# Two groups of attention outputs in one PSUM bank, and a round of seven banks for all other jobs

## The chip, the cores and the metric

The kernel runs on one core of one Trainium2 chip. The metric is the device time of one execution in microseconds (us); lower is better. The names of the engines are those of the profile: PE is the matrix engine (PEld its weight loads), DVE the vector engine, ACT the scalar engine, POOL the third elementwise engine, SP the queue that issues DMAs. PSUM is the memory that PE writes its results to; the program holds it as one tensor `ps` of 128 partitions, 8 banks and 512 float32 values in each bank.

## The reference, cut to what matters

The input `x` is 8 images of 256 channels and 16x16 pixels. A non-local block and a quantised convolution block come first. Then the pixels become 256 tokens of 256 channels for each image, and four residual layers follow:

```python
t = t + _L2_attn_ref(_ln_t(t), L2_attn_w_in, L2_attn_b_in, L2_attn_w_out, L2_attn_b_out)
t = t + _L2_ffn_ref(_ln_t(t), L2_ffn_weight)
t = t + _L3_attn_ref(_ln_t(t), L3_attn_w_q, L3_attn_w_k, L3_attn_w_v, L3_attn_w_o)
t = t + _L3_ffn_ref(_ln_t(t), L3_ffn_We, L3_ffn_be, L3_ffn_Wr, L3_ffn_br, L3_ffn_Wo, L3_ffn_bo)
```

Both attentions are causal, with 16 heads of 16 channels:

```python
scores = jnp.einsum('bhqd,bhkd->bhqk', q, k) / math.sqrt(dh)   # the first one adds an alibi bias
scores = jnp.where(causal, scores, -inf)
attn = jax.nn.softmax(scores, axis=-1)
out = jnp.einsum('bhqk,bhkd->bhqd', attn, v)
```

The change touches only how the last line of this, the product of the softmax weights with V, is held in PSUM and copied out, and how many banks all other products of these four layers share.

## The kernel before

The first part of the program (the two convolution blocks, about 0 to 115 us) is not touched. The second part works through 16 bodies: 8 images through the first attention and its feed-forward layer (stages 0 and 1), then 8 images through the second attention and the mixture of experts (stages 2 and 3). A body is a list of pieces `(kind, stage, batch, n)`, each with a step in time; a body begins 12 steps after the one before, so that three or four images are under way at once. `in_order("tensor")` gives the order in which PE does the pieces, `in_order("others")` the order for ACT, DVE, POOL and SP. Each engine takes its pieces strictly in this order, and waits on semaphores.

The pieces, as far as the text needs them:

- `LNa`, `LNb`: the layer norm on DVE (statistics L1364 to L1370, and `xn` at L1375), with one power on POOL between them (L1079). `T`: PE turns `xn` around (L1119), ACT copies it to `xnT` (L1277).
- `Q`, `K`, `V` (L1127, L1135): the projections, taken out by ACT (L1291, L1294) and DVE (L1385, L1388, L1410, L1412).
- The 16 heads are 4 groups of 4. `S` (3 per group): scores, of which DVE takes the maximum (`nmax`, L1419). `MS`: DVE splits the maximum (L1428, L1429). `M`: PE turns it (L1183), ACT copies it into `QS` (L1306). `X` (3 per group): scores again, transposed and with the maximum taken off (L1194 begins them, L1198 ends them); ACT takes the exponential into `PT` (L1312).
- `O0` and `O1` (L1209, L1216): the product of V with `PT` for group n, with a row of sums. Four matmuls of 32 rows each fill the 128 partitions, 256 columns wide. ACT copies these to `OT` (L1316). `OX` (L1223): PE turns `OT` back, and DVE divides by the sums into `attn` (L1435, L1436).
- `AT`, `PR`: `attn` turned (L1119) and copied by ACT, projected (L1135) and added to the residual by DVE (L1446). `FF`: the feed-forward product (L1135), also added at L1446.
- `R`, `RT`, `GT`, `GB`, `E` (8 per image, L1252), `CT`: the router, its gates (transposed by PE at L1241, copied by ACT into `gateT` at L1327, used by PE at L1246), the experts, which DVE scales and adds up two by two (`acc`, L1499), and the output.

PSUM is shared as follows. All kinds in `JOBS` (all products named above but `O0` and `O1`) take a bank in turn, `self.bank[p] = jobs % RING` with `RING = 6`. Before it writes, PE waits until the previous job in the same bank is copied out, that is the job six places back in its own order: `drained(pe, piece, 1)`. Banks 6 and 7 are for the attention outputs, bank `6 + n % 2` for group n. Both groups of a pair (0 and 1, 2 and 3) stand at the same step, behind each other: `O0` and `O1` of the even group, then `O0` and `O1` of the odd one; their `OX` come two steps later.

Of the kernel before, what the change touches and what calls it, by code (L numbers as in the profile page):

```python
# [9 lines left out]
ACT = mybir.ActivationFunctionType  # L10
# [5 lines left out]
PIX = IMG * IMG  # L16
# [8 lines left out]
GROUPS = 4  # L25
# [37 lines left out]
                   ("br", 2 * EXPERTS))  # L63

UNITS = 3 * GROUPS
RING = 6

# [96 lines left out]
def signals(piece, bank):  # L166

    kind, n = piece[0], piece[3]
    out = []
    if kind in JOBS:  # L170
        out += [(f"bank_full{bank}", 1), (f"bank_drained{bank}", 1)]
    if kind == "O1":
        out += [(f"bank_full{6 + n % 2}", 1), (f"bank_drained{6 + n % 2}", 1)]
    if kind in SETTLED:
        out.append(("dve_step", settled(piece)))
    out += {"LNa": [("var_ready", 1), ("rstd_ready", 1)], "LNb": [("xn_ready", 1)], "XB": [("x_biased", 1)],
            "MS": [("max_split", 1)], "PAD": [("own_rows", 1), ("padded", 4), ("chosen", 1), ("chosen_spread", 16 * (STACKS - 1))], "CT": [("out_stored", 16)],
            "Q": [("first_ready0", 1)], "K": [("first_ready1", 1)],
            "SPLIT": [(f"second_ready{n}", 1), (f"third_ready{n}", 1), (f"parts_stored{n}", 16)],
            "LOAD": [(f"stack_loaded{n}", 16 * (len(Q_PARTS) + (piece[1] == 0 and n == 0)))],  # L180
            "R": [("router_shifted", 1)], "RT": {0: [("router_exp", 1)], 3: [("gates_ready", 1)]}.get(n, [])}.get(kind, [])
    return out
# [22 lines left out]
COUNTS = Counts()  # L205


def build(nc, x_in, fix_in, fixb_in, bias_in, w0_in, w1_in, wt_in, wm_in, parts_dram, out):
    ctx = ExitStack()
    with ctx:  # L210
# [6 lines left out]
        ps = ctx.enter_context(nc.psum_tensor("ps", [P, 8, 512], F32))  # L217
# [714 lines left out]
        with ExitStack() as c2:  # L932
# [23 lines left out]
            OT = lb("OT", [P, 2, PIX])  # L956
# [25 lines left out]
            def bank_number(piece):  # L982

                if piece is None:
                    return None
                return 6 + piece[3] % 2 if piece[0] == "O1" else COUNTS.bank.get(piece)

            def full(eng, piece):

                wait(eng, f"bank_full{bank_number(piece)}", piece)  # L990

            def drained(eng, piece, less=0):

                wait(eng, f"bank_drained{bank_number(piece)}", piece, less)
# [7 lines left out]
            def flat(ap):  # L1002
                return ap.rearrange("p a n -> p (a n)")
# [25 lines left out]
            def earlier_unit(kind, stage, batch, n, by, per):  # L1029

                return previous(kind, stage, batch, (n - by) % per, (by - n + per - 1) // per)
# [74 lines left out]
            def tensor_piece(pe, piece):  # L1106
# [6 lines left out]
                mm = None  # L1113
# [85 lines left out]
                                       QS[r, at, 4 * g + j, kt * P:], start=False, stop=(k == len(heads) - 1),  # L1199
                                       skip_group_check=True)  # L1200
                if kind == "O0":
                    o = ps[:, 6 + n % 2, :]
                    drained(pe, ("X", stage, batch, 3 * n))
                    drained(pe, ("X", stage, batch, 3 * n + 1))
                    if n == 0:
                        drained(pe, ("V", stage, batch, 0))
                    drained(pe, ("O1", stage, batch, n), 1)
                    for j in range(4):
                        pe.matmul(o[32 * j:32 * j + 32, 0:PIX], V[:, at, 0, 4 * n + j, :],  # L1209
                                  PT[:, pt_slot(piece, 3 * n + j // 2), (j % 2) * PIX:(j % 2 + 1) * PIX],  # L1210
                                  start=True, stop=False, skip_group_check=True)
                if kind == "O1":
                    o = ps[:, 6 + n % 2, :]
                    drained(pe, ("X", stage, batch, 3 * n + 2))
                    for j in range(4):
                        mm = pe.matmul(o[32 * j:32 * j + 32, P:PIX], V[:, at, 1, 4 * n + j, :],  # L1216
                                       PT[:, pt_slot(piece, 3 * n + 2), j * P:(j + 1) * P],
                                       start=False, stop=True, skip_group_check=True)
                    mm.then_inc(sems[f"bank_full{6 + n % 2}"], 1)
                if kind == "OX":  # L1220
                    drained(pe, ("O1", stage, batch, n))
                    for t in range(2):
                        mm = pe.transpose(d[:, t * P:(t + 1) * P], OT[:, n % 2, t * P:(t + 1) * P], F("ident"))  # L1223
                if kind == "AT":
# [46 lines left out]
            def scalar_piece(act, piece):  # L1271
# [37 lines left out]
                if kind == "X":  # L1309
                    full(act, piece)  # L1310
                    pt_free(act, piece)
                    act.activation(PT[:, pt_slot(piece, n), :], bank(piece), ACT.Exp).then_inc(drain(piece), 1)  # L1312
                if kind == "O1":
                    full(act, piece)
                    full(act, earlier_unit("OX", stage, batch, n, 2, GROUPS))
                    act.activation(OT[:, n % 2, :], ps[:, 6 + n % 2, 0:PIX], ACT.Copy)\  # L1316
                        .then_inc(sems[f"bank_drained{6 + n % 2}"], 1)
                if kind == "AT":
                    full(act, piece)
                    full(act, ("PR", stage, batch - 1, 0))  # L1320
# [15 lines left out]
            def pt_free(eng, piece):  # L1336

                earlier = earlier_unit("X", *piece[1:], PT_RING, UNITS)
                if earlier:
                    full(eng, ("O1", *earlier[1:3], earlier[3] // 3))  # L1340


            def vector_piece(dve, piece):
# [332 lines left out]
```

## Time and profile before

| what | value |
|---|---|
| median of 3 runs | 665.81 us (664.83 to 666.66) |
| the profiled execution's own time | 665.75 us |
| its span, first to last instruction | 664.0 us |
| around the span | 1.75 us |
| granted clock of PE, mean | 0.964 |
| PE busy | 593.3 us (89%) |
| DVE busy | 447.8 us (67%) |
| ACT busy | 326.7 us (49%) |

A granted clock of 1 is 2.4 GHz, 0.5 is 1.2 GHz. An engine's idle time matters where the chain of work that ends last runs through it.

### The profile page before, as it was taken

The page shows a single profiled execution, that of the slowest core. Times are in us where ns is not written, and L with a number is a line of the kernel's source. Part 1 is how long each engine was busy: PE and PEld are TensorE (multiplying, and loading weights), DVE is VectorE, ACT ScalarE, POOL GpSimd, SP SyncE. Part 2 cuts the span into 40 slices and gives each one's busy share as a digit, 9 for nine tenths or more (in the row PEclk, how much of TensorE's full clock was granted, in tenths as well). Part 3 has the DMA queues.
Part 4 walks back from the last instruction along what each step waited for, and adds up shares of the span by engine and source line. Part 5 has one row for each costly group of instructions (what it writes and reads, how often), then busy time and mean ns, then how long its engine had stood idle before and what let it go on. Part 6 is the DMA issues. An engine that isn't in the chain of part 4 may idle for free.

```text
span 664.0 us, 11227 instructions
## 1 busy us (share of the span) xinstructions
PE 593.3 (89%) x4159; PEld 407.7 (61%) x4206; DVE 447.8 (67%) x1275; ACT 326.7 (49%) x548; POOL 117.8 (18%) x115
## 2 busy tenths in 40 slices
PE   5884776768999999999999979999999999999897
PEld 2653334656767767767767757576675756565443
DVE  4767858758477577677677584776858576676464
ACT  2436658617566566566566554343443535353110
POOL 2031000260313313303303302011030200000000
PEclk9985998789899999999999988999999999999999
DMA  9500000375134134134134141204040230000000
GB/s 335 216 0 0 1 0 6 82 212 168 50 99 146 44 107 146 33 116 139 37 113 138 30 120 55 89 25 135 1 142 18 62 98 17 1 17 0 17 13 19
DMA packets 40253, 50.64 MB, mean 76 GB/s; under 512 B 4052, under 2 KB 33492, under 8 KB 39892
## 3 DMA queue, kind: packets, MB, share of 16 engines
q1 hardware_dynamic: 40200, 49.94, 24.3%
q8 instruction: 33, 0.54, 0.4%
q14 instruction: 20, 0.16, 0.1%
HBM read 35.11 MB, written 14.68 MB: 75 GB/s over the span
## 4 chain that ended last, share of the span: by engine, by line
PE 60%; DVE 15%; issue 3%; ACT 2%; DMA 1%; SPq 1%; POOL 0%; DVEq 0%; ACTq 0%
PE ps L1252 14%; PE ps L1135 8%; PE ps L1127 7%; PE ps L1209 5%; PE ps L1198 5%; DVE nmax L1419 4%; PE ps L1119 4%; PE ps L1194 3%; PE ps L1178 3%; PE ps L1170 3%; PE ps L1216 2%; DVE acc L1499 2%; PE ps L1173 2%; DVE xn L1375 2%; DVE stats L1364 2%
## 5 line engine op out<-in xcount | busy, mean ns | idle before, releaser
L1419 DVE TENSOR_REDUCE nmax<-ps 128x2 f32<-128x512 f32 (+1 forms) x192 | 130.7, 687 | 79.5 <-PE ps L1178 52.1
L1312 ACT ACTIVATE PT<-ps 128x512 f32<-128x512 f32 x192 | 113.3, 598 | 115.7 <-PE ps L1198 114.0
L1252 PE MATMUL ps<-wm,xnT 128*128 128x512 f32 x256 | 119.9, 599 | 0.7
L1079 POOL TENSOR_TENSOR rstd<-ve,fix 128x2 f32<-128x2 f32 x32 | 22.2, 695 | 321.6 <-DVE ve L1370 321.6
L1306 ACT ACTIVATE QS<-ps 8x1024 bf16<-8x1024 f32 x64 | 65.1, 1017 | 27.3 <-PE ps L1183 25.3
L1198 PE MATMUL ps<-QS,KS 110*128 110x256 bf16 (+3 forms) x512 | 74.7, 247 | 0.0
L1499 DVE SCALAR_TENSOR_TENSOR acc<-ps,gate,acc 128x256 f32<-128x256 f32 x128 | 61.6, 481 | 18.5 <-PE ps L1252 16.2
L1252 PEld LDWEIGHTS ps<-wm,xnT 128*128 128x128 f32 x256 | 45.1, 190 | 39.7 <-issue 38.1
L1127 PE MATMUL ps<-xnT,by_dim 128*128 128x256 f32 x256 | 63.4, 394 | 2.2 <-ACT xnT L1277 2.2
L1099 POOL TENSOR_TENSOR parts<-rest,fix 128x512 bf16<-128x512 f32 x30 | 38.1, 1270 | 139.8 <-DVE rest L1388 100.5
L1194 PE MATMUL ps<-fixb 128*128 128x256 bf16 (+1 forms) x192 | 60.0, 312 | 2.3 <-DVE nmax L1419 2.0
L1127 PEld LDWEIGHTS ps<-xnT,by_dim 128*128 128x128 f32 x256 | 48.0, 197 | 8.8 <-ACT xnT L1277 2.1
L1198 PEld LDWEIGHTS ps<-QS,KS 110*128 110x128 bf16 (+1 forms) x512 | 45.2, 98 | 11.9 <-issue 1.7
L1178 PE MATMUL ps<-KS,QS 110*128 110x256 bf16 (+1 forms) x256 | 50.1, 277 | 0.0
L1135 PE MATMUL ps<-wt,xnT 128*128 128x256 f32 x192 | 45.8, 381 | 0.0
L1209 PE MATMUL ps<-PT,V 128*32 128x256 f32 x512 | 41.9, 400 | 0.0
L1135 PEld LDWEIGHTS ps<-wt,xnT 128*128 128x128 f32 x192 | 34.8, 190 | 4.1
L1173 PE MATMUL ps<-fixb 128*128 128x256 bf16 x128 | 35.7, 279 | 1.0 <-DVE rest L1385 1.0
L1103 POOL TENSOR_TENSOR parts<-rest,parts 128x512 bf16<-128x512 f32 x30 | 34.7, 1157 | 2.4
L1178 PEld LDWEIGHTS ps<-KS,QS 110*128 110x128 bf16 (+1 forms) x256 | 25.6, 100 | 12.4 <-issue 8.3
L1277 ACT ACTIVATE xnT<-ps 128x512 f32<-128x512 f32 x32 | 19.1, 597 | 27.8 <-PE ps L1119 27.8
L1119 PE MATMUL ps<-fix,xn 128*128 128x128 f32 x128 | 21.2, 290 | 12.9 <-DVE xn L1375 11.6
(211 smaller groups left out, 925.9 us busy)
## 6 DMA issues: line engine op xcount, KB each, us to landing
parts_dram<-parts SPq DMA_DIRECT2D x32, 384.0 KB, 3.0
QS<-parts_dram SPq DMA_DIRECT2D x96, 128.0 KB
KS<-parts_dram SPq DMA_DIRECT2D x96, 128.0 KB, 2.6
wt<-wt_dram SPq DMA_DIRECT2D x1, 2562.0 KB, 19.5
wm<-wm_dram SPq DMA_DIRECT2D x1, 2449.0 KB, 14.0
xc<-x_dram SPq DMA_DIRECT2D x8, 256.0 KB, 5.7
out_dram<-res SPq DMA_DIRECT2D x8, 256.0 KB, 2.1
w<-w_dram SPq DMA_DIRECT2D x1, 845.0 KB, 8.8
```

Source lines behind the costliest of these rows:

```text
L1127: mm = pe.matmul(d[:, o * PIX:(o + 1) * PIX], w[:, c, o], src[:, c, :], start=(c == 0), stop=(c == 1))
L1135: mm = pe.matmul(d[:, t * width:(t + 1) * width], src[:, c, t * P:(t + 1) * P], w[:, c * wstep + w_at:c * wstep + w_at + width], start=(c ...
L1173: pe.matmul(d.rearrange("p (j k n) -> p j k n", j=2, k=2)[:, :, 1, :], FB("ident"), FB("tri1").rearrange("p (j n) -> p j n", j=2), start=T ...
L1178: mm = pe.matmul(d[:, jj * PIX:(jj + 1) * PIX], QS[r, at, h, P:2 * P], KS[r, at, h, :], start=False, stop=(jj == 1), skip_group_check=True)
L1194: pe.matmul(d.rearrange("p (j n) -> p j n", n=width)[:, :, 0:P], FB("tri0", 0, P), FB("ident").unsqueeze(1).broadcast_to([P, len(heads), P ...
L1198: mm = pe.matmul(d[:, k * width:(k + 1) * width], KS[r, at, 4 * g + j, kt * P:(kt + 1) * P], QS[r, at, 4 * g + j, kt * P:], start=False, s ...
L1209: pe.matmul(o[32 * j:32 * j + 32, 0:PIX], V[:, at, 0, 4 * n + j, :], PT[:, pt_slot(piece, 3 * n + j // 2), (j % 2) * PIX:(j % 2 + 1) * PIX ...
L1252: mm = pe.matmul(d, normT(stage, batch)[:, c, t * P:(t + 1) * P], M("We", c * EXPERTS * CH + e * 2 * CH, 2 * CH), start=(c == 0), stop=(c ...
L1306: act.activation(QS[MAX_AT:MAX_AT + MAX_ROWS, stack(stage, batch), 4 * n:4 * n + 4, :], bank(piece)[MAX_AT:MAX_AT + MAX_ROWS, 0:PIX].unsqu ...
L1312: act.activation(PT[:, pt_slot(piece, n), :], bank(piece), ACT.Exp).then_inc(drain(piece), 1)
L1419: dve.tensor_reduce(group[:, 0, :] if part == 0 else group[:, 1, 2 * part - 2:2 * part], bank(piece).rearrange("p (j n) -> p j n", n=w_), ...
L1499: op = dve.scalar_tensor_tensor(acc[:, t, :], bank(piece)[:, k * CH:(k + 1) * CH], gate[:, par, t, 2 * e + k:2 * e + k + 1], acc[:, t, :], ...
```

## The change

The attention outputs of the two groups of a pair now lie in one bank, number 7 (`O_BANK`): the even group in columns 0 to 255, the odd group in columns 256 to 511. PE signals once, behind the odd group's `O1`, and ACT makes one copy of 128x512 in place of two of 128x256. `OX` of the even group, the reuse of the bank and the reuse of `PT` slots wait for the pair's signal. Bank 6 goes into the round of the other jobs, so that a job waits for the one seven places back.

```diff
-RING = 6
+RING = 7
+O_BANK = 7
...
-    if kind == "O1":
-        out += [(f"bank_full{6 + n % 2}", 1), (f"bank_drained{6 + n % 2}", 1)]
+    if kind == "O1" and n % 2:
+        out += [(f"bank_full{O_BANK}", 1), (f"bank_drained{O_BANK}", 1)]
...
-                return 6 + piece[3] % 2 if piece[0] == "O1" else COUNTS.bank.get(piece)
+                return O_BANK if piece[0] == "O1" else COUNTS.bank.get(piece)
+
+            def pair(stage, batch, n):
+
+                return "O1", stage, batch, n | 1
...
                 if kind == "O0":
-                    o = ps[:, 6 + n % 2, :]
+                    o = ps[:, O_BANK, n % 2 * PIX:(n % 2 + 1) * PIX]
                     drained(pe, ("X", stage, batch, 3 * n))
                     drained(pe, ("X", stage, batch, 3 * n + 1))
                     if n == 0:
                         drained(pe, ("V", stage, batch, 0))
-                    drained(pe, ("O1", stage, batch, n), 1)
+                    drained(pe, pair(stage, batch, n), 1)
...
                 if kind == "O1":
-                    o = ps[:, 6 + n % 2, :]
+                    o = ps[:, O_BANK, n % 2 * PIX:(n % 2 + 1) * PIX]
...
-                    mm.then_inc(sems[f"bank_full{6 + n % 2}"], 1)
+                    if n % 2:
+                        mm.then_inc(sems[f"bank_full{O_BANK}"], 1)
                 if kind == "OX":
-                    drained(pe, ("O1", stage, batch, n))
+                    drained(pe, pair(stage, batch, n))
...
-                if kind == "O1":
+                if kind == "O1" and n % 2:
                     full(act, piece)
+                    full(act, earlier_unit("OX", stage, batch, n, 3, GROUPS))
                     full(act, earlier_unit("OX", stage, batch, n, 2, GROUPS))
-                    act.activation(OT[:, n % 2, :], ps[:, 6 + n % 2, 0:PIX], ACT.Copy)\
-                        .then_inc(sems[f"bank_drained{6 + n % 2}"], 1)
+                    act.activation(flat(OT), ps[:, O_BANK, :], ACT.Copy).then_inc(sems[f"bank_drained{O_BANK}"], 1)
...
                 earlier = earlier_unit("X", *piece[1:], PT_RING, UNITS)
                 if earlier:
-                    full(eng, ("O1", *earlier[1:3], earlier[3] // 3))
+                    full(eng, pair(*earlier[1:3], earlier[3] // 3))
```

## Rows read from the trace of the kernel before

**Rows 1.** The page: busy time of engines, and PE's granted clock in 40 slices.

```profile
PE 593.3 (89%) x4159; PEld 407.7 (61%) x4206; DVE 447.8 (67%) x1275; ACT 326.7 (49%) x548; POOL 117.8 (18%) x115
...
PEclk9985998789899999999999988999999999999999
```

**Rows 2.** Busy time by windows of 32 us: stage 0, then the experts twice.

```profile
core 0: us, PE busy (x) PEld busy (x) DVE busy (x) ACT busy (x) POOL busy (x), PEclk, DMA share, GB/s
...
300.00:332.00 32.00, 31.09 (x260) 24.37 (x263) 21.64 (x63) 18.66 (x30) 11.07 (x10) 1.00 0.30 91
460.00:492.00 32.00, 31.54 (x205) 21.73 (x206) 22.27 (x70) 13.78 (x24) 5.55 (x5) 1.00 0.14 42
```

**Rows 3.** Waits of PE's weight loads: total us, times, longest us.

```profile
PEld ps L1119 <- DVE nmax L1419: 3.2, 8, 0.4
PEld ps L1183 <- DVE nmax L1419: 3.2, 8, 0.4
...
PEld ps L1194 <- DVE nmax L1419: 2.3, 2, 1.3
...
PEld ps L1194 <- DVE attn L1436: 1.7, 8, 0.2
PEld ps L1194 <- DVE X L1446: 1.7, 8, 0.2
...
PEld ps L1252 <- DVE acc L1499: 1.1, 5, 0.2
```

**Rows 4.** Waits of PE's matmuls, the longest in total.

```profile
PE ps L1119 <- DVE xn L1375: 11.6, 16, 3.1
```

**Rows 5.** DVE's timeline in one body of stage 0: start, duration, [idle before].

```profile
307.65 0.69 DVE L1419 TENSOR_REDUCE nmax<-ps 128x4 f32<-128x512 f32 x1 [0.92 <-PE ps L1170]
...
317.11 0.73 DVE L1375 TENSOR_SCALAR xn<-X,mv,rstd 128x256 f32<-128x256 f32 x2
...
318.35 0.68 DVE L1446 TENSOR_TENSOR X<-ps,X 128x512 f32<-128x512 f32 x1
...
332.80 0.69 DVE L1419 TENSOR_REDUCE nmax<-ps 128x4 f32<-128x512 f32 x1 [0.92 <-PE ps L1170]
```

**Rows 6.** PE's timeline in the same body, matmuls alone.

```profile
317.98 0.63 PE L1119 MATMUL ps<-fix,xn 128*128 128x128 f32 x4 [0.41 <-DVE xn L1375]
...
319.98 0.40 PE L1216 MATMUL ps<-PT,V 128*32 128x128 f32 x8
320.20 0.61 PE L1209 MATMUL ps<-PT,V 128*32 128x256 f32 x8
```

**Rows 7.** ACT's groups, shapes kept apart: busy, mean ns, idle before.

```profile
L1316 ACT ACTIVATE OT<-ps 128x256 f32<-128x256 f32 x64 | 21.5, 384 | 6.4 <-PE ps L1216 6.4
L1277 ACT ACTIVATE xnT<-ps 128x512 f32<-128x512 f32 x32 | 19.1, 597 | 27.8 <-PE ps L1119 27.8
```

**Rows 8.** DVE's timeline, then PE's, in one body with experts.

```profile
464.42 0.69 DVE L1419 TENSOR_REDUCE nmax<-ps 128x4 f32<-128x512 f32 x1 [0.94 <-PE ps L1170]
...
473.35 0.73 DVE L1375 TENSOR_SCALAR xn<-X,mv,rstd 128x256 f32<-128x256 f32 x2
...
474.23 0.63 PE L1119 MATMUL ps<-fix,xn 128*128 128x128 f32 x4 [0.22 <-DVE xn L1375]
```

**Rows 9.** DVE's timeline in a late body, where no norm of a later image follows.

```profile
546.42 0.69 DVE L1419 TENSOR_REDUCE nmax<-ps 128x2 f32<-128x512 f32 x1 [0.48 <-PE ps L1178]
```

**Rows 10.** ACT's and PE's timelines behind the last pair of groups.

```profile
618.73 0.39 ACT L1316 ACTIVATE OT<-ps 128x256 f32<-128x256 f32 x1 [0.27 <-PE ps L1216]
619.07 0.39 ACT L1327 ACTIVATE gateT<-ps 128x256 f32<-128x256 f32 x1
...
619.50 0.48 PE L1246 MATMUL ps<-wm,gateT 128*128 128x256 f32 x1 [0.47 <-ACT gateT L1327]
```

**Rows 11.** Busy time and granted clock by windows around one fall of the clock.

```profile
162.80:166.25 3.45, 1.34 (x13) 0.85 (x11) 3.17 (x11) 1.43 (x3) 1.30 (x2) 1.00 0.00 0
166.25:169.66 3.41, 3.41 (x33) 1.97 (x34) 0.69 (x1) 2.60 (x4) 0.68 (x1) 0.50 0.00 0
```

## The prediction

> **What bounds the kernel now.** I read the page first: PE is busy 89% of the span, DVE 67%, ACT 49% [rows 1]. Then the windows of 32 us: in stage 0 PE is busy 31.1 of 32, with experts 31.5 of 32, always at a granted clock of 1.00, which is 2.4 GHz [rows 2]. So in the second part of the program PE has under 1 us of idle time in 32, and the change can only win some of that; it takes no work from PE. The third view is the one to which the change speaks: what PE waits for, by the instruction that released it [rows 3]. Its weight loads show short waits on readers of PSUM that repeat 8 times, once a body. Set beside the order of the jobs, each is a wait for the bank six places back: `T` of stage 1 for an `S` (0.4 us each), `M` of group 0 for an `S` (0.4), the last `X` of an image for an `OX` (0.2), the second `X` of the next image for `FF` (0.2), and with experts the fifth `E` for the fourth (5 times 0.2). With the two singular ones (2.3) they sum to 3.2 + 3.2 + 2.3 + 1.7 + 1.7 + 1.1 = 13.2 us. The largest wait of all is another: `T` for `xn`, 11.6 us in 16 [rows 4]. That is data, and no bank shortens it.
>
> So I asked in one body of stage 0 which engine sets the time of each stretch. DVE waits for PE 0.92 us and starts the first `nmax` of an image at 307.65. From there it works without waiting for PE to the end of `xn` at 317.11 + 0.73 = 317.84, and PE's `T` comes 0.14 later, at 317.98, having waited [rows 5, 6]. The same start of an image comes again at 332.80, again after DVE had waited 0.92 for PE [rows 5]. A body thus has two stretches: 10.3 us set by DVE (307.65 to 317.98), then 14.8 us set by PE (317.98 to 332.80), 25.15 in all. A wait of PE in the first stretch costs nothing; one in the second costs its length.
>
> **The seventh bank.** Of the four waits of a body, three lie in the DVE stretch: those of `T`, `M` and the last `X`. If they go, PE is up to 0.4 + 0.4 + 0.2 us earlier at the next `T`, and `xn` is as late as it was: the wait moves to rows 4. I count them 0; their cover is the 10.3 us of DVE, and without it they would bring 3.2 + 3.2 + 1.7 = 8.1. One lies in the PE stretch: the second `X` of the next image waits for DVE's addition of `FF`, 318.35 + 0.68 = 319.03 [rows 5]. With seven banks it waits for the job before that, the last `X` of the image ahead, which ACT took out before the `T` at 317.98. That is 1.7 us in 8 bodies [rows 3], and DVE's next start, being set by PE, follows. **-1.7.**
>
> Bodies with experts: the fifth `E` waits 0.22 (1.1 in 5). In three of them DVE is again without a wait from 464.42 to the `xn` at 474.08, and `T` follows at 474.23 after a wait [rows 8], so 0. In the two late bodies no image follows that needs a norm, and DVE itself waits 0.48 for PE behind that `E` [rows 9]; there it counts. **-0.4.** The two singular waits (2.3) lie between stages and in the first bodies, before a `T` that waits for `xn` in any case (up to 3.1, [rows 4]): 0.
>
> Could seven banks make some wait longer? A job waits for the bank seven places back, and PE has already waited for that bank at its previous job in the old round, so the new condition is never later than the old ones together. POOL and SP touch no bank; `SPLIT` and the DMAs behind it follow `Q` and `K`, which shift with PE.
>
> **The copy.** Two copies of 128x256 at 384 ns become one of 128x512. That shape with the same operation takes 597 ns [rows 7]. ACT is spared 32 x (768 - 597) = 5.5 us of work, which at 49% busy is worth nothing by itself. But the one copy begins when the second began and ends 597 - 384 = 0.21 us later. Who waits: `OX`, two steps and over 1 us behind `O1` in every body, so 0. Behind the copy in ACT's order stand exponentials whose `X` PE has not finished, 0, and in the late bodies `gateT`. In the last one ACT goes straight from the copy (618.73 + 0.39) to `gateT` at 619.07, and PE's `GB` waits 0.47 for it [rows 10]: +0.2 in full. In the two bodies before, PE has other work between, and I charge 0.1 each, between 0 and 0.2. **+0.4.**
>
> **The rest.** The semaphore waits that fall away (an even group's full and drained signals) stood before instructions that had nothing left to wait for: 0. The `PT` slots are reused 9 units later; ACT has by then waited for the pair to copy it: 0. The even group's bank is now held until the pair's copy, and the next pair comes 6 steps later, half a body or 12.6 us, so no wait.
>
> **Sum.** -1.7 - 0.4 + 0.4 = -1.7 us: a span of 662.3, an own time of 664.05. The profiled execution (665.75) stands 0.06 under the median, so the median becomes 664.1. The body of stage 0 goes from 25.15 to 24.94.
>
> **A rule weighed.** The page "Perfetto Trace Analysis" of the Trainium skill, section Identifying Performance Opportunities, says that the same gap repeating on the engine that should be saturated can mean too few PSUM buffers. The trace agrees that the gaps repeat and that a bank ends them; it does not show that they set the pace. By the rule all 13.2 would come back, which is rival A.
>
> **Rivals.**
>
> A. *More of the waits comes back.* For it: if DVE's stretch were not rigid, say because PE's earlier results let DVE's pieces overlap better, `xn` would come earlier too. Against it: DVE shows no wait for PE in those 10.3 us [rows 5]. All of rows 3 would give 665.8 - 13.2 + 0.4 = 653; half of it 659.6.
>
> B. *The clock.* The waits of PE gather before `T`: about 1.3 us in one body of stage 0, most of it in one piece, where now they are spread. For it: before the fall at 166.25 PE was busy only 1.34 of 3.45 us, and then ran 3.41 us at 0.50, which is 1.2 GHz [rows 11]; that costs half, 1.7 us. Against it: in a stage-0 body PE would still be busy most of any such stretch, and today's scattered waits never bring it down there [rows 2]. The Trainium skill, "TensorE: Matmul & The Clock Gate", section on psum-queue depth-cycling, tells of a kernel whose short idles from cycling through banks made the clock oscillate; this trace, cycling through six banks at 1.00, does not agree. Once a body it would be 8 x 1.7 = 13.6: 677.7; from three bodies on the result is slower (+5.1 - 1.7 = +3.4).
>
> C. *One bank for two groups costs PE.* Now the odd group's `O0` starts at 320.20 while the even group's `O1` ends at 319.98 + 0.40 = 320.38, into another bank [rows 6]. If PE had to let the first end before it writes the same bank, each pair costs 0.18 us. For it: no pair of groups shows this order within one bank. Against: within one group `O1` follows `O0` in the same bank, and two halves of a bank are written back to back by every `OX` and `FF`. Of 32 pairs some 9 lie in a DVE stretch; 23 x 0.18 = 4.1 gives 668.2. It ends slower than before by over 0.3% from 0.16 us a pair on.
>
> D. *Nothing moves.* The 0.2 behind `FF` is given back at the next product that waits for ACT: 665.4 to 666.2.
>
> **How the numbers follow.** 0.3% (2.0 us) is about what a measurement of this kernel can tell from no change; the three runs lie within 1.8. My forecast, a gain between 1 and 2.6 us, has 0.58; of that 0.23 beyond 2.0 and 0.35 within. A has 0.17, all faster. D has 0.11, the same. C has 0.08 and B 0.06, slower. So faster 0.40, same 0.46, slower 0.14. The range reaches down to 658.5, which takes in the half of A, and up to 667.5, which takes in most of C's span of prices; the far part of A and B lie outside. The likeliest case alone is 663.2 to 664.8.
>
> **What the profile after would show.** Right: the waits of weight loads for L1446 and for `nmax` (the two that come 8 times) are gone, one for `attn` before the last `X` may stay, and the wait of `T` for `xn` has grown from 11.6 to some 17 to 19 us; DVE's stretch from first `nmax` to `xn` is still 10.2 us; the body is 24.94; `OT` copies are 32 of about 597 ns; `GB` at the end waits 0.2 longer. Wrong: a shorter DVE stretch (A), 0.50 in the windows of stage 0 (B), the odd `O0` later than 0.68 behind the even one (C). The forecast fails most easily if what ends DVE's stretch is not DVE, or if the single falls of the clock in the first bodies and between the stages land elsewhere: one more or less of 3.4 us is 1.7 us, as much as the whole gain.

## The result, and the profile after

| | before | changed |
|---|---|---|
| median, timed side by side on one chip, 7 runs each | 664.83 us (664.3 to 666.66) | 660.72 us (660.13 to 663.51) |
| the profiled execution's own time | 665.75 us | 660.13 us |
| its span | 664.0 us | 658.3 us |
| granted clock, mean | 0.964 | 0.971 |

The ratio is 0.994, with an interval of 0.9927 to 0.9954: faster by 4.1 us, beyond the 0.3% that a measurement can tell. I had forecast 1.7 us. The sign was right, the size less than half of it.

The page of the changed kernel, busy time and granted clock in 40 slices:

```profile
PE 590.1 (90%) x4206; PEld 408.4 (62%) x4206; DVE 447.8 (68%) x1275; ACT 325.9 (50%) x516; POOL 117.7 (18%) x115
...
PEclk9985998798899999999999999999999999999999
```

PE has the same work. Beside [rows 1] the clock row has lost the two slices of 8 in its second half, 382 to 415 us of the span of before, between the stages. The falls of its first 11 slices are the same in both, of the same lengths and within 0.2 us of the same times; that one 8 stands a slice later is only the narrower slice of a shorter span.

PE's waits after the change, weight loads first, then matmuls (total us, times, longest us):

```profile
PEld ps L1124 <- DVE xn L1381: 9.8, 9, 3.2
...
PEld ps L1199 <- DVE nmax L1425: 3.3, 8, 0.4
```

```profile
PE ps L1124 <- DVE xn L1381: 15.1, 16, 3.1
...
PE ps L1188 <- DVE nparts L1435: 4.8, 1, 4.8
...
PE ps L1199 <- DVE nmax L1425: 1.9, 8, 0.2
```

(The lines stand 5 to 6 lower than before: L1124 is `T`, L1188 `M`, L1199 the start of `X`, L1214 and L1221 are `O0` and `O1`, L1323 the `OT` copy, L1425 `nmax`, L1381 `xn`, L1452 the addition to `X`; in the kernels below that have an added line they stand one lower again.) Of the bank waits of [rows 3] those of `T` for `nmax` and those for `attn`, for `X` and for `acc` are gone. The one of `M` has only moved a job on. `M` of group 0 needed the bank of the `S` six places back; with seven banks the job behind it, the last `X` but one of the image ahead, needs the bank of that same `S`, and now this `X` waits for the same `nmax`, again 8 times and up to 0.4 us (3.3 us in all, where `M` had 3.2). That part was not won at all. And `T` waits longer for `xn`, 15.1 us where [rows 4] had 11.6.

One body of stage 0, DVE first (start, duration, what; idle before in brackets):

```profile
306.02 0.69 DVE L1425 TENSOR_REDUCE nmax<-ps 128x4 f32<-128x512 f32 x1 [0.99 <-PE ps L1175]
...
315.47 0.73 DVE L1381 TENSOR_SCALAR xn<-X,mv,rstd 128x256 f32<-128x256 f32 x2
...
316.72 0.69 DVE L1452 TENSOR_TENSOR X<-ps,X 128x512 f32<-128x512 f32 x1
...
330.89 0.69 DVE L1425 TENSOR_REDUCE nmax<-ps 128x4 f32<-128x512 f32 x1 [0.99 <-PE ps L1175]
```

Then PE, its matmuls:

```profile
311.89 0.28 PE L1199 MATMUL ps<-fixb 128*128 128x256 bf16 x1 [0.24 <-DVE nmax L1425]
...
316.26 0.66 PE L1124 MATMUL ps<-fix,xn 128*128 128x128 f32 x4 [0.54 <-DVE xn L1381]
317.20 0.27 PE L1199 MATMUL ps<-fixb 128*128 128x256 bf16 x1
317.62 0.64 PE L1214 MATMUL ps<-PT,V 128*32 128x256 f32 x8
318.07 0.40 PE L1221 MATMUL ps<-PT,V 128*32 128x128 f32 x8
318.29 0.61 PE L1214 MATMUL ps<-PT,V 128*32 128x256 f32 x8
```

From the first `nmax` to the end of `xn` is 306.02 to 316.20 = 10.18 us; in [rows 5] it was 10.19. This is the rigid stretch that I had named: DVE has no wait for PE in it, and taking PE's waits out of it has not made it shorter. The PE stretch, from `T` at 316.26 to DVE's next start at 330.89, is 14.63 us where [rows 5, 6] had 14.82, and there the second `X` (317.20) goes out without a wait. With `T` 0.08 nearer to the end of `xn`, the body is 24.87 us instead of 25.15: 0.28 less, and I had said 0.21. The odd group's `O0` starts 0.67 us behind the even one (318.29 against 317.62) while the even group's `O1` is still on, and both now write one bank. So rival C has no price.

A late body, DVE behind the fifth `E`:

```profile
540.72 0.69 DVE L1425 TENSOR_REDUCE nmax<-ps 128x2 f32<-128x512 f32 x1 [0.19 <-PE ps L1183]
```

DVE waits 0.19 us where [rows 9] had 0.48; I find each of the two late bodies 0.24 us shorter. The end of the program, ACT and then PE behind the last pair of groups:

```profile
612.84 0.60 ACT L1323 ACTIVATE OT<-ps 128x512 f32<-128x512 f32 x1 [4.36 <-PE ps L1221]
613.33 0.38 ACT L1333 ACTIVATE gateT<-ps 128x256 f32<-128x256 f32 x1
...
613.86 1.10 PE L1252 MATMUL ps<-wm,gateT 128*128 128x256 f32 x4 [0.71 <-ACT gateT L1333]
```

`GB` waits 0.71 us for `gateT` where [rows 10] had 0.47: the longer copy costs 0.24 there, forecast 0.2.

None of this makes 5.6 us, the difference of the two profiled executions. The largest part lies between the stages. Windows of the kernel before around that place (columns as in [rows 2]), rows that were not shown above:

```profile
391.50:394.95 3.45, 0.96 (x9) 0.43 (x6) 2.98 (x12) 2.81 (x5) 0.42 (x1) 1.00 0.00 0
394.95:401.78 6.83, 6.29 (x49) 4.02 (x50) 2.97 (x12) 3.29 (x6) 0.00 (x0) 0.50 0.01 2
```

The same place in the changed kernel:

```profile
389.50:393.00 3.50, 0.50 (x4) 0.23 (x3) 3.15 (x12) 2.55 (x4) 0.00 (x0) 1.00 0.00 0
393.00:399.00 6.00, 5.95 (x64) 4.76 (x65) 3.44 (x12) 3.81 (x7) 0.00 (x0) 1.00 0.01 3
```

In both kernels PE has little to do for some 3.5 us (two waits, of 1.1 and 1.9 us) while DVE and ACT bring the first results of stage 2. Before, the granted clock was then 0.50, that is 1.2 GHz, for 6.83 us; after, it stayed at 1.00, 2.4 GHz. From the start of each job of PE in the two traces, the changed kernel gains 2.95 us between the stages, 2.05 in stage 0, 0.5 in the late bodies, and gives back 0.33 at the end; the three bodies with experts before the late ones take as long as they did; the first 115 us, which the change does not touch, came out 0.4 shorter. Sum: 2.95 + 2.05 + 0.5 - 0.33 + 0.4 = 5.6.

PE's idle stretch itself is the same in both. Before, then after, the two waits of which it consists (start of the first matmul behind the wait, length of the wait in brackets):

```profile
393.08 0.27 PE L1194 MATMUL ps<-fixb 128*128 128x256 bf16 x1 [1.11 <-DVE nmax L1419]
...
395.49 0.90 PE L1119 MATMUL ps<-fix,xn 128*128 128x128 f32 x3 [1.92 <-DVE xn L1375]
```

```profile
390.62 0.27 PE L1199 MATMUL ps<-fixb 128*128 128x256 bf16 x1 [1.11 <-ACT QS L1312]
...
393.05 0.63 PE L1124 MATMUL ps<-fix,xn 128*128 128x128 f32 x4 [1.94 <-DVE xn L1381]
```

So the seventh bank has neither filled this stretch nor changed its lengths, though what ends the first wait is now ACT's `QS` and no longer an `nmax`; the stretch stands 2.46 us earlier (idle from 389.51 instead of 391.97).

### The profile page after: what moved, and what is told of

Same layout as the page of the kernel before. It is cut to its first block, busy times and chain, and to the rows that moved or that the text cites. A ratio compares the mean times of both kernels' runs of the same rounds, so it can differ in the third digit from the quotient of the medians.

```text
span 658.3 us, 11240 instructions
## 1 busy us (share of the span) xinstructions
PE 590.1 (90%) x4206; PEld 408.4 (62%) x4206; DVE 447.8 (68%) x1275; ACT 325.9 (50%) x516; POOL 117.7 (18%) x115
## 4 chain that ended last, share of the span: by engine, by line
PE 56%; DVE 18%; issue 3%; ACT 1%; DMA 1%; POOL 1%; SPq 1%; DVEq 0%; ACTq 0%
PE ps L1258 14%; PE ps L1140 9%; PE ps L1132 8%; DVE nmax L1425 5%; PE ps L1203 4%; PE ps L1214 4%; PE ps L1124 4%; PE ps L1183 3%; DVE xn L1381 3%; PE ps L1199 2%; DVE stats L1370 2%; DVE acc L1505 2%; PE ps L1221 2%; PE ps L1178 2%; PE ps L1175 1%
## 5 line engine op out<-in xcount | busy, mean ns | idle before, releaser
L1425 DVE TENSOR_REDUCE nmax<-ps 128x2 f32<-128x512 f32 (+1 forms) x192 | 130.6, 686 | 74.5 <-PE ps L1183 46.9
L1199 PE MATMUL ps<-fixb 128*128 128x256 bf16 (+1 forms) x192 | 59.7, 311 | 3.0 <-DVE nmax L1425 1.9
L1214 PE MATMUL ps<-PT,V 128*32 128x256 f32 x512 | 41.0, 393 | 0.0
L1124 PE MATMUL ps<-fix,xn 128*128 128x128 f32 x128 | 20.4, 283 | 15.1 <-DVE xn L1381 15.1
```

The lines of the kernel that those rows point to most:

```text
L1199: pe.matmul(d.rearrange("p (j n) -> p j n", n=width)[:, :, 0:P], FB("tri0", 0, P), FB("ident").unsqueeze(1).broadcast_to([P, len(heads), P ...
L1425: dve.tensor_reduce(group[:, 0, :] if part == 0 else group[:, 1, 2 * part - 2:2 * part], bank(piece).rearrange("p (j n) -> p j n", n=w_), ...
```

## The experiments

Two theories stood against each other for the 2.95 us. *Placement*: the fall of the clock between the stages happens or not by where in time PE's idle stretch comes to lie; the change has moved it by about 2 us and has had luck. *Shape*: with seven banks the stretch itself is different, so that the clock holds, or more of the bank waits come back there (rival A in that place alone).

Each batch has its own runs of the kernel before on the same chip; their medians are 664.91 (27 runs), 665.59 (23), 665.34 (17) and 665.27 (17), and 664.83 beside the changed kernel. A difference between two batches is therefore uncertain by up to 0.8 us. A delay of the second part is made by clearing the unused `acc` on DVE ahead of the first body, 0.66 us for each whole clearing with its wait; this is work added, and nothing that is computed changes.

**The copy alone.** Pairs share a bank, the round stays at six:

```diff
-RING = 7
+RING = 6
```

> One bank for the two groups and one copy, but the round of the other jobs stays at six; bank 6 lies unused. If the seventh bank is what gives the time: as before, ratio to before 0.999 to 1.001, body of stage 0 25.15 us, span about 664, with the stretch at 1.2 GHz at some 395 us still there. If the merged copy is what gives it: body 25.0 or less, ratio under 0.998. If one bank for two groups costs PE (rival C of the prediction): each pair up to 0.18 us, ratio up to 1.006.

Measured: 665.58 us (664.4 to 667.29), ratio 1.0014 (1.0002 to 1.0025). Waits of PE's weight loads, a stage-0 body by DVE's starts:

```profile
PEld ps L1124 <- DVE nmax L1425: 3.2, 8, 0.4
PEld ps L1188 <- DVE nmax L1425: 3.2, 8, 0.4
...
PEld ps L1199 <- DVE X L1452: 1.7, 8, 0.2
```

```profile
307.00 0.69 DVE L1425 TENSOR_REDUCE nmax<-ps 128x4 f32<-128x512 f32 x1 [0.93 <-PE ps L1175]
...
332.13 0.69 DVE L1425 TENSOR_REDUCE nmax<-ps 128x4 f32<-128x512 f32 x1 [0.93 <-PE ps L1175]
```

The waits of [rows 3] are back to the tenth, and the body is 25.13 us. The pair in one bank with its one copy costs 0.7 us at the median (forecast +0.4, inside the interval of 0.1 to 1.7) and gains nothing. So what the structure gains is the seventh bank's, and C is out a second time. The clock fell between the stages here too, for 3.41 us, half as long as in the kernel before, although this kernel also has six banks in the round.

**The changed kernel later, the kernel before later.** Four whole clearings and one half (3.0 us by DVE's rows; the bodies of the profiled execution stand 3.2 later), and three clearings (2.0 us); the first as a diff, the second has `range(3)`:

```diff
+            delayed = sem("delayed")
...
+                    for k in range(5):
+                        dve.memset(acc[:] if k < 4 else acc[:, 0], 0.0).then_inc(delayed, 1)
+                        dve.wait_ge(delayed, k + 1)
```

> The changed kernel with DVE clearing a tile five times (some 2.4 us) before the first body, so that the bodies stand where they stood in the kernel before. Placement theory (the stretch at 1.2 GHz at 395 us went because PE's idle time between the stages came 2.5 us earlier after the start): it comes back, 660.7 + 2.4 + 3.0 = 666, slower than before. Shape theory (seven banks make the idle time of another shape and so keep the clock up): it stays away, 663.1.

> The kernel before with the same clearing three times (some 1.6 us) ahead of the first body, nothing else. Placement theory: the stretch at 1.2 GHz at 395 us goes or becomes shorter, 664.8 + 1.6 - 3.0 = 663.4, or 665 if half of it goes; faster than before although it does more. Shape theory, and the theory that the clock does not depend on the time: 664.8 + 1.6 = 666.4, with the stretch in the trace.

Measured: the changed kernel 663.3 us (661.57 to 664.18), ratio 0.9974 (0.9964 to 0.9984): no fall between the stages, and 2.6 us for 3.0 of delay, as shape had forecast (663.1). The kernel before 666.27 us (663.19 to 669.02), ratio 1.0023 (1.0007 to 1.0038): 1.4 us for 2.0 of delay, with an interval of 0.5 to 2.5. The median alone does not contradict a clock that takes no notice of the delay (forecast 666.4), and it misses the 663.4 to 665 of placement. In its profile the clock was 0.50 for only half as long as undelayed:

```profile
397.62:401.03 3.41, 3.41 (x24) 2.21 (x28) 2.40 (x9) 2.06 (x3) 0.00 (x0) 0.50 0.00 0
```

In this pair of traces the bodies stand 2.1 us later up to 380 us and 0.7 later from 402 us on. The length of the fall thus can change where nothing but a delay was added, which speaks for placement. It does not settle it, since the changed kernel held its clock.

**The norms of later images one step earlier in DVE's order**, on the changed kernel: if `T` waits for `xn`, bring `xn` forward.

```diff
-    0: (("LNa", 0, 0, -21), ("LNb", 0, 0, -19),
+    0: (("LNa", 0, 0, -22), ("LNb", 0, 0, -20),
...
-    2: (("LNa", 2, 0, -21), ("LNb", 2, 0, -19),
+    2: (("LNa", 2, 0, -22), ("LNb", 2, 0, -20),
```

> The changed kernel with LNa and LNb of stages 0 and 2 one step earlier in the order of DVE and POOL. If the stretch of a body up to T's wait for xn is set by the order of DVE, T comes up to 0.9 us earlier, its wait of 0.7 us goes, and 8 bodies win 0.3 to 0.7 each: 655 to 658.5. If DVE's sum of work sets it, whatever the order, the wait goes to the next piece that needs a maximum (M or X) and the time stays at 660.7.

Measured: 660.44 us (659.37 to 661.11), ratio 0.9935 (0.992 to 0.9951), the changed kernel's own time. The stage-0 body is 25.25 us, 0.39 longer, and PE's timeline says where:

```profile
315.69 0.28 PE L1199 MATMUL ps<-fixb 128*128 128x256 bf16 x1 [1.38 <-DVE nmax L1425]
```

This is the `X` behind `M` again, with its seven-banks-back `S`. The norm has overtaken that `S`'s maximum, the bank comes free later, and the wait has grown from 0.24 to 1.38 us. This order of DVE does not help in this stretch: DVE has no wait in it, and what went ahead pushed back another thing that PE needs. Bodies with experts gain 0.85 us each, and 1.0 is won between the stages (the expectation of the run with both changes below says 2.0; by DVE's starts the stretch went from 29.87 to 28.89). 8 x 0.39 lost and 3 x 0.85 + 1.0 won nearly cancel.

**More delays, to catch the fall.** The changed kernel with four clearings (2.6 us); the kernel before with one (0.66 us):

> The changed kernel with the clearing four times, 2.6 us by the rows of e2, where five had shifted the bodies by 3.2 and the changed kernel's clock was seen at the same point as without a shift. Placement theory: with this shift PE's idle time between the stages falls where it fell in the kernel before, against the moments at which the clock can change; the stretch at 1.2 GHz at some 395 us comes back in most runs, mean clock 0.964 to 0.967, 660.7 + 2.6 + 2 to 3 = 665.5 to 666.5. Shape theory (seven banks keep it away): clock 0.969 or more, 663.3.

> The kernel before with the clearing once, 0.66 us. Placement theory: PE's idle time between the stages falls, against the moments at which the clock can change, where it falls in the changed kernel; the stretch at 395 us goes, mean clock 0.969 or more, 664.9 + 0.7 - 2 to 3 = 662.6 to 663.6, faster than before. Shape theory: clock as before (0.963 to 0.968), 665.5.

Measured: the changed kernel 664.03 us (662.27 to 667.37), ratio 0.9995 (0.9977 to 1.0014). Its 12 runs lie in two groups: 8 at a granted clock of 0.968 with spans of 660.3 to 662.4 us, and 4 at 0.962 to 0.964 with 665.2 to 665.4. Neither forecast fits the median: the fall came back, but not in most runs. The profiled one is of the second group, and has the fall with seven banks:

```profile
395.89:402.72 6.83, 5.57 (x46) 3.56 (x47) 3.48 (x14) 2.70 (x5) 0.00 (x0) 0.50 0.01 2
```

The kernel before with one clearing: 666.19 us (664.64 to 667.73), ratio 1.0011 (0.9998 to 1.0024). Here placement had forecast that the fall would go, and it did not:

```profile
395.41:402.24 6.83, 5.90 (x47) 3.75 (x48) 3.33 (x14) 2.98 (x5) 0.00 (x0) 0.50 0.01 2
```

**`T` one step later in PE's order**, on the changed kernel. If `T` blocks PE's queue for `xn` while an `X` behind it could go, put the `X` ahead:

```diff
-("T", 0, 0, -18)
+("T", 0, 0, -17)
...
-("T", 2, 0, -18)
+("T", 2, 0, -17)
```

> The changed kernel with T of stages 0 and 2 one step later in PE's order (behind S, M, X and the products with V of that step), DVE's order untouched. If the end of DVE's stretch matters only because T stands at the head of PE's queue, PE does some 3 us of other work while it waits, T's wait for xn (0.7 in 8 bodies, 0.4 in those with experts) goes: 5 to 7 us less, 654 to 656. If DVE's stretch holds PE by other ways too (a maximum for M, a bank for X), the wait moves and the time stays within 1 us of 660.7.

Measured: 656.99 us (655.35 to 657.46), ratio 0.9872 (0.985 to 0.9894), 3.7 us under the changed kernel. `T` in PE's timeline, the wait in the waits of matmuls, and the body by DVE's starts:

```profile
316.73 0.65 PE L1124 MATMUL ps<-fix,xn 128*128 128x128 f32 x4
```

```profile
PE ps L1124 <- DVE xn L1381: 4.6, 3, 3.1
```

```profile
304.88 0.69 DVE L1425 TENSOR_REDUCE nmax<-ps 128x4 f32<-128x512 f32 x1 [0.92 <-PE ps L1175]
...
329.23 0.69 DVE L1425 TENSOR_REDUCE nmax<-ps 128x4 f32<-128x512 f32 x1 [0.92 <-PE ps L1175]
```

`T` waits for nothing, 15.1 us of waiting has become 4.6, and the body is 24.35 us, 0.52 less. So `T` for `xn` was where the two stretches joined. The size missed its forecast of 5 to 7 us. The trace shows a part of what is missing: ahead of the first image a projection now waits 4.5 us for `xnT`, and the first `nmax` starts at 149.45 instead of 145.40, of which 2.5 come back in the next two bodies.

**Both: `T` later, and the norms earlier in the expert bodies alone.**

```diff
+                step -= s == 2 and b >= 4 and kind in ("LNa", "LNb")
```

> e7 and, for the images 4 to 7 of stage 2, whose norms stand in the bodies with experts, LNa and LNb one step earlier. In e4 that gave 0.85 us in each of three such bodies and 2.0 between the stages, and cost 0.39 in each body of stage 0, which is left out here. If the two add: e7's time less 2 to 4 us. If T's later place already takes those waits: e7's time.

Measured: 654.8 us (654.41 to 655.57), ratio 0.9846 (0.9823 to 0.9869). An expert body is 38.11 us in the profile where the kernel before had 38.97. This kernel beats both, the one before by 10.8 us and the changed one by 5.9. The 2.2 us against the kernel with `T` alone later lie in the forecast, but in the traces the earlier norms gain only 0.7 us: an expert body has 38.35 us without them. The rest of the difference of the two traces, 1.7 us, goes with a fall of 3.41 us at 613.6, late in the program, which only the kernel without them has.

**Two clearings before the kernel before** (1.3 us), once more for placement:

> The kernel before with the clearing twice, 1.3 us. In seven traces of this idle stretch the clock fell for 3.4 us when the fall came 3.2 us or more after PE went idle, for 6.8 us when it came 2.3 to 3.0 us after, and not at all in two traces that lie further along the same way. Placement theory: a shift of 1.3 us puts the kernel before there; no stretch at 1.2 GHz near 395 us in most runs, mean clock 0.969 or more, 664.9 + 1.3 - 2.5 = 663.7. Against it: clock 0.968 or less, 666.2.

Measured: 667.08 us (665.27 to 668.72), ratio 1.0026 (1.0014 to 1.0039). The fall stayed at its full length, a second miss for that forecast:

```profile
393.61:400.43 6.82, 5.65 (x46) 3.60 (x47) 3.48 (x14) 3.07 (x6) 0.00 (x0) 0.50 0.00 0
```

**What the bank is worth where `T` does not wait.** The kernel before with `T` one step later, and the best kernel with six banks (`RING = 6`):

> The kernel before (six banks, two output banks) with T of stages 0 and 2 one step later, as e7. If DVE's stretch was the cover that made three of the four bank waits of a body free, they come out now: against e7 (657.0) it loses them and the wait behind FF, up to 0.9 in each of 8 bodies, 660 to 664. If the later T gives the same with six banks: its gain of 3.7 is kept, 661 with the 1.7 of the banks and the clock's share, and not more.

> e8 with the round of the other jobs at six, bank 6 unused: the worth of the seventh bank where T and the norms no longer hold PE. Cover theory: more than the 2.2 us that the seventh bank gives in the changed kernel, 4 to 7 us, 659 to 662. If the bank waits were covered by other things too: 2 us, 657.

Measured: 658.99 us (657.93 to 660.02), ratio 0.991 (0.9894 to 0.9925), for the first, and 659.95 us (657.76 to 660.5), ratio 0.9917 (0.99 to 0.9933), for the second. The first one's stage-0 body, by DVE's starts, and its bank waits:

```profile
304.71 0.69 DVE L1419 TENSOR_REDUCE nmax<-ps 128x4 f32<-128x512 f32 x1 [0.99 <-PE ps L1170]
...
329.26 0.69 DVE L1419 TENSOR_REDUCE nmax<-ps 128x4 f32<-128x512 f32 x1 [0.78 <-PE ps L1170]
```

```profile
PEld ps L1119 <- DVE nmax L1419: 3.2, 8, 0.4
PEld ps L1183 <- DVE nmax L1419: 3.2, 8, 0.4
```

24.55 us against 24.35 with seven banks: 0.20 a body, the same number as in the pair before, but not for the same wait. The one behind `FF`, which had counted there, is gone from this kernel's list: with `T` behind the second `X`, the job six places back of this `X` is the last `X` of the image ahead and no longer `FF`. The three that had been free are all there. `T` starts without a wait:

```profile
316.76 0.66 PE L1119 MATMUL ps<-fix,xn 128*128 128x128 f32 x4
```

From the first `nmax` to this `T` it is 12.05 us (304.71 to 316.76), with seven banks 11.85 (304.88 to 316.73); from `T` to the next first `nmax` it is 12.50 in both. So the 0.20 is what the three formerly covered waits cost once `T` no longer waits for `xn`. In the bodies with experts, where the seventh bank had been worth 0.00, it is worth 0.47 here (38.82 against 38.35 us). The kernels differ by 2.0 us at their medians, under both forecasts (660 to 664, and 661). This six-bank kernel also lost time at 1.2 GHz: its fall between the stages, at 390.18, lasts 3.41 us, and its six runs have clocks of 0.969 to 0.971.

In the second pair the two kernels differ by 659.95 - 654.8 = 5.1 us. Its expert body, and then the same of the kernel with seven banks:

```profile
449.48 0.69 DVE L1426 TENSOR_REDUCE nmax<-ps 128x4 f32<-128x512 f32 x1 [2.71 <-PE ps L1176]
...
488.01 0.69 DVE L1426 TENSOR_REDUCE nmax<-ps 128x4 f32<-128x512 f32 x1 [2.71 <-PE ps L1176]
```

```profile
445.25 0.69 DVE L1426 TENSOR_REDUCE nmax<-ps 128x4 f32<-128x512 f32 x1 [2.71 <-PE ps L1176]
...
483.37 0.69 DVE L1426 TENSOR_REDUCE nmax<-ps 128x4 f32<-128x512 f32 x1 [2.71 <-PE ps L1176]
```

38.53 against 38.12 us: 0.41 in each of three bodies, where the change as made gave 0.00. With 0.22 in a stage-0 body, 0.36 in each of the two late ones and 1.8 between the stages this makes 5.5; 0.2 more come from the first 115 us, and 0.6 are given back at the end: 5.1, the difference of the two traces. Most of the 1.8 is not the bank's: the six-bank kernel's profile has a fall of 3.41 us there, which can cost up to 1.7, the other's has none. By the mean clocks of the runs (41.7 and 38.7 us at 1.2 GHz, worked out as below) the clock has up to 1.5 of the 5.1, so the bank is worth some 3.5 here and not 5.1.

**The delay that decides.** The changed kernel with three clearings (2.0 us). Its idle stretch then begins at 391.4 us, in the kernel before at 392.0:

> The changed kernel with the clearing three times, 2.0 us. Two forecasts of the placement theory (e6, e9) failed on the kernel before, whose clock kept falling wherever the bodies stood; on the changed kernel one shift left the clock up (e2) and one brought the fall back in part (e5). Placement theory: at 2.0 us the fall at some 395 us comes in most runs, mean clock 0.967 or less, 661 + 2.0 + 2 to 3 = 665 to 666. Shape theory (something in the seven-bank order keeps the clock up in most runs): mean clock 0.969 or more, 663.

Measured: 664.97 us (662.87 to 666.2), ratio 0.9993 (0.9979 to 1.0008). Windows between the stages, and a stage-0 body by DVE's starts:

```profile
389.90:393.60 3.70, 1.95 (x19) 1.21 (x16) 3.31 (x16) 2.49 (x5) 0.69 (x1) 1.00 0.12 35
393.60:400.43 6.83, 5.53 (x46) 3.51 (x47) 3.47 (x14) 2.70 (x5) 0.00 (x0) 0.50 0.01 2
```

```profile
307.88 0.69 DVE L1426 TENSOR_REDUCE nmax<-ps 128x4 f32<-128x512 f32 x1 [0.99 <-PE ps L1176]
...
332.75 0.69 DVE L1426 TENSOR_REDUCE nmax<-ps 128x4 f32<-128x512 f32 x1 [0.99 <-PE ps L1176]
```

The body is the changed kernel's, 24.87 us; seven banks, and the fall is there at its full 6.83 us. 2.0 us of delay has cost 664.97 - 660.72 = 4.25 (two batches, so uncertain by the 0.8 named above). The pair of profiles is sharper: from the first `nmax` of the last stage-0 image to that of the first stage-2 image it is 32.46 us where the changed kernel has 29.87, so 2.6 us are lost in that one place, and every later body is the changed kernel's to 0.01. Eight of the 12 runs have a granted clock of 0.962 to 0.964; of the changed kernel's seven, none. The shape of the seven-bank schedule does not keep the clock up.

The nine traces in which PE's idle stretch has the same form (1.1 and then 1.9 us) can be laid side by side. The last column is the length from the last stage-0 image's first `nmax` to the next image's:

| kernel, delay | PE idle from | clock falls at | behind it | at 1.2 GHz | stretch |
|---|---|---|---|---|---|
| changed, 0 | 389.51 | none | | 0 | 29.87 |
| changed, 3.0 | 392.73 | none | | 0 | 29.87 |
| changed, 2.0 | 391.36 | 393.60 | 2.24 | 6.83 | 32.46 |
| changed, 2.6 | 393.61 | 395.89 | 2.28 | 6.83 | 32.48 |
| before, 1.3 | 391.26 | 393.61 | 2.35 | 6.83 | 32.51 |
| before, 0.66 | 392.82 | 395.41 | 2.59 | 6.83 | 32.63 |
| before, 0 | 391.97 | 394.95 | 2.98 | 6.83 | 32.82 |
| pair alone, 0 | 391.29 | 394.48 | 3.19 | 3.41 | 31.30 |
| before, 2.0 | 394.05 | 397.62 | 3.57 | 3.41 | 31.47 |

Six and seven banks stand in one series: what the stretch costs goes with how far behind the start of the idling the fall comes, and not with the number of banks. Where it comes 2.28 us behind it with seven banks and 2.35 with six, the stretches differ by 0.03. Both traces without a fall are of the changed kernel; no profile of a six-bank kernel with this stretch lacks it, though the unchanged kernel before has once run at a clock of 0.974, in 661.91 us. The table also shows what the two failed forecasts of placement had missed. The profiled execution with two clearings has its idle stretch 0.7 us earlier than the kernel before, not 1.3 later, because its first 115 us ran 1.2 shorter; and against the fall the delays moved it only from 2.98 to 2.59 and 2.35, where the fall still has its full length.

This run also gives the bank's own worth. Time at 1.2 GHz is about 2 x (1 - clock) x span: 46.0 us here on the mean, 46.1 in the 17 runs of the kernel before beside it, 40.5 in the changed kernel's seven. Half of a difference in it is the most that it can cost, since PE is not always busy in it. With the clocks alike, the difference that is left is structure (the 2.0 is the program's own delay): 665.27 + 2.0 - 664.97 = 2.3 us.

## Why the prediction was off by more than half

**What bounds a body** held to the hundredth: 10.3 us set by DVE and 14.8 set by PE, joined at `T`. The DVE stretch kept its length, the PE stretch lost the wait behind `FF`. What moved in PE's waits had been named: the wait of `T` for `xn` grew. It went to 15.1 us and not to 17 to 19; I take as the reason that the wait of `M` never fell away: it stands one job on, at an `X`. I had reasoned rightly that seven banks make no wait later than the old ones together, and had not followed it to its other half, that a wait can be handed to the next job in full. In this stretch that made no difference to the time.

**The seventh bank, -1.7 in eight bodies** came out at -2.05 in the pair of profiles. The fall-away of the wait is 0.19 of each body's 0.28; the rest is `T` 0.08 closer behind `xn`, for which I had no term. **-0.4 in the two late bodies** came out at -0.5. **0 in the three bodies with experts** came out at 0.00, and the reason given was right: with the cover gone, the same bank is worth 0.41 to 0.47 in each.

**The copy, +0.4**: 597 ns as forecast, 0.33 at the end by the traces, 0.7 at the medians with its interval of 0.1 to 1.7.

**Structure together** was forecast at -1.7 and measured at -2.2 in the pair of traces and -2.3 where the clocks are alike.

**The step that failed** is the 0 that I wrote for the waits between the stages, as if nothing there could move the time, and with it the treatment of the clock. I had looked for a fall only in the bodies (rival B, which never came) and mentioned the stretches between the stages as a thing that "lands elsewhere", without a term, a sign or a chance in the sum. The trace of before had a stretch of 6.83 us at 0.50 at 394.95, which my text never looked at: [rows 11] show the one at 166. Its price in the pair of traces is 2.95 us, more than the whole structural gain, and by the mean clocks 46.1 - 40.5 = 5.6 us less at half speed, so at most 2.8. The measured 4.1 is thus 2.3 of banks and about 2 of a fall that mostly did not happen; the split is good to some 0.8 us, the spread between batches.

**Luck.** 660.7 lies in the range of 658.5 to 667.5, but not for the reasons in it. The sum itself gave 664.1, and its likeliest case ended at 663.2; the part of the range that holds 660.7 had been opened for half of rival A, and A did not happen. That the fall stayed away came from where the change moved PE's idle stretch, which I had not forecast.

**The rivals.** A: in stage 0 the DVE stretch is as long as it was, so none of the covered waits came back; C: the two `O0` stand 0.67 us apart, and the copy alone lost nothing beyond its 0.7; B: the granted clock is 1.00 from 170 to 656 us, over all of stage 0 and the experts; D: the 0.2 behind `FF` was kept in every body.

**A weighed rule.** The Trainium skill, "Perfetto Trace Analysis", Identifying Performance Opportunities, reads repeating gaps on the saturated engine as a possible sign of too few PSUM buffers. The traces agree for 2.3 of the 13.2 us of such gaps, and for some 3.5 once `T` and the norms had been moved; for the rest another engine set the pace. The Trainium skill, "TensorE: Matmul & The Clock Gate", Part 1, says that the same kernel can see its low-clock time vary from run to run. The 12 runs with four clearings agree: eight at 0.968 with times of 662.3 to 664.4 us, four at 0.962 to 0.964 with 666.9 to 667.4.

**My "without cover 8.1"** was much too high. With `T` free of `xn`, the three covered waits of a stage-0 body were worth 0.20 together, 1.6 us in 8 bodies. One of them, 3.2 of the 8.1 us, a seventh bank does not remove but hands on. Of the 0.6 of the other two (`T` for an `S`, the last `X` for an `OX`) those 0.20 came back; I suppose that the maxima that `M` and `X` need from the same full DVE cover the rest, but have not taken that apart.

**What stays open.** Where the fall will come against the idle stretch can't be told ahead from a delay: the first 115 us of the traces differ by up to 1.7 us, and by their clocks four of 12 runs with four clearings had the fall, and eight of 12 with three. Placement forecast the wrong outcome twice; by the table the stretch had not moved far enough against the fall. What is shown: the changed kernel has the fall or not by a delay of 2 us with nothing else changed, and the kernels before stand in the same series, so its 2 us of clock are no property of seven banks; whether another program that places this stretch otherwise keeps them can't be told ahead.

## What to carry to other kernels

Before a bank wait is given a price, find which engine sets the stretch in which it lies: here one wait in four counted; two turned into a wait for data, and one was handed to the next job in the round. When another change moves that stretch, price the waits again: with `T` later the one that had counted was gone, and the others began to cost. When PE stands blocked on data at the head of its queue, put independent work ahead of it: moving one `T` by one step won 3.7 us on the changed kernel, at nearly the same mean clock. The 6.4 us that it won on the one before are not all its own: its runs have 39.0 us at 1.2 GHz where the kernel before has 46.8, so up to 3.9 of them are the clock's. When a difference of half a per cent comes with a different mean clock, delay one of the kernels by a microsecond or two before crediting the change with it.

## What the runs showed of the hardware

A delay of 2.0 us ahead of the second part cost 4.25 us, 2.6 of them in one place, since PE's idle stretch of some 3.5 us then ended in 6.83 us at 1.2 GHz; a delay of 3.0 us cost 2.6. In nine traces with the same idle stretch the fall either did not come (twice), came 2.2 to 3.0 us behind its start and lasted 6.83 us (five times), or came 3.2 to 3.6 behind it and lasted 3.41 (twice), with six banks as with seven. Two groups written into one bank, one starting while the last instructions of the other are under way, run at the pace of two banks (0.67 against 0.68 us from one `O0` to the next).
